# A four-layer attention kernel: queries of a quad projected in one piece, two norm statistics moved to another slot

## What is computed

```python
# block 0: self-attention with rotary q and k, a 128x128 mask; then cross-attention to 77 context tokens; then an MLP
x = x + g_msa * (attn(rope(q), rope(k), v, mask) @ attn_out_W)   # "l0", 128 keys, 16 heads of 8
x = x + g_x * (attn(qc, kc, vc, kv_mask) @ co_W)                 # "l0c", 77 keys
x = x + g_mlp * mlp(adaLN(x))
# block 1: routed experts over x and an attention to the context ("routed")
# block 2: cross-attention to 77 context tokens                    "l2"
# block 3: self-attention "l3s" (128 keys, no mask), cross-attention "l3c" (77 keys), MLP
```

## Time and profile before

| | |
|---|---|
| median of 3 runs | 1057.93 us (1056.93 to 1058.32) |
| the profiled execution | 1056.9 us |
| its span | 1055.1 us |
| mean granted TensorE clock | 0.985 of full |
| TensorE busy | 1011.1 us, 96% |
| VectorE, ScalarE, GpSimd busy | 773.0, 602.4, 677.2 us |

### The profile page before, as it was taken

One profiled execution on the slowest core, in us unless ns is written; L12 is line 12 of the kernel. 1 busy time (PEld: TensorE's weight loads), 2 busy tenths in 40 slices (PEclk: granted clock), 3 DMA queues, 4 the chain that ended last, 5 costly groups with the idle time before them and its releaser, 6 DMA issues.

```text
span 1055.1 us, 28781 instructions
## 1 busy us (share of the span) xinstructions
PE 1011.1 (96%) x11721; PEld 639.5 (61%) x11721; DVE 773.0 (73%) x1932; ACT 602.4 (57%) x858; POOL 677.2 (64%) x779
## 2 busy tenths in 40 slices
PE   7899999999999999999999799999999999999998
PEld 5345555656655776666776555655556666665576
DVE  7889988778885443777787779888998867777421
ACT  2144444566767455455554466666666677666762
POOL 6688888687985333111114689987889767688620
PEclk9699999999999999999999899999999999999999
DMA  6300000000000102000000000000000000000011
GB/s 218 119 2 2 21 14 13 12 22 22 12 22 22 40 31 99 13 7 8 7 7 19 7 14 2 2 2 2 1 2 2 1 3 2 2 2 2 2 40 40
DMA packets 9282, 22.76 MB, mean 22 GB/s; under 512 B 1392, under 2 KB 1648, under 8 KB 8768
## 3 DMA queue, kind: packets, MB, share of 16 engines
q1 hardware_dynamic: 9152, 20.94, 5.7%
HBM read 18.77 MB, written 2.15 MB: 20 GB/s over the span
## 4 chain that ended last, share of the span: by engine, by line
PE 81%; DVE 10%; issue 4%; ACT 2%; POOL 2%; DMA 0%; SPq 0%; DVEq 0%; POOLq 0%; ACTq 0%
PE weighed L707 13%; PE scores L679 11%; PE row_scores L642 8%; PE scores L903 6%; PE weighed L730 5%; DVE negmax L1221 5%; PE quads L578 4%; PE scores L597 4%; PE quads L589 3%; PE scores L692 3%; PE row_scores L903 3%; PE quads L604 3%; PE row_scores L720 2%; PE scores L720 2%; PE weighed L920 2%
## 5 line engine op out<-in xcount | busy, mean ns | idle before, releaser
L1221 DVE TENSOR_REDUCE negmax<-row_scores 128x8 f32<-128x616 f32 (+1 forms) x312 | 298.8, 958 | 80.2 <-PE row_scores L642 62.3
L1730 ACT ACTIVATE p<-scores 128x1024 f32<-128x1024 f32 (+1 forms) x253 | 249.1, 1019 | 159.4 <-PE scores L692 131.9
L679 PE MATMUL scores<-qblk,work 32*77 32x512 f32 (+1 forms) x1256 | 203.8, 612 | 5.0 <-ACT p L1730 3.3
L1912 POOL TENSOR_TENSOR kblk_r<-work,pack_const 128x308 fp32r<-128x308 f32 (+1 forms) x160 | 133.6, 836 | 64.5 <-PE row_scores L642 48.7
L707 PE MATMUL weighed<-p,v 77*32 77x128 f32 (+1 forms) x5120 | 172.9, 276 | 0.3
L1902 POOL TENSOR_TENSOR qblk<-work,pack_const 128x512 f32<-128x512 f32 x160 | 166.0, 1038 | 0.0
L642 PE MATMUL row_scores<-kblk_r,qr 32*128 32x308 f32 (+1 forms) x624 | 141.6, 445 | 20.1 <-DVE negmax L1221 16.9
L707 PEld LDWEIGHTS weighed<-p,v 77*32 77x32 f32 (+1 forms) x5120 | 130.1, 109 | 36.8 <-issue 29.0
L642 PEld LDWEIGHTS row_scores<-kblk_r,qr 32*128 32x128 f32 x624 | 62.0, 186 | 107.5 <-issue 69.6
L1949 POOL TENSOR_TENSOR attn<-nat,rden 128x128 f32<-128x128 f32 x160 | 65.6, 410 | 55.6 <-DVE rden L1251 54.5
L692 PE MATMUL scores<-nblk,select 32*77 32x512 bf16 (+1 forms) x628 | 95.4, 375 | 0.0
(11 more groups left out here) (327 smaller groups left out, 1868.6 us busy)
## 6 DMA issues: line engine op xcount, KB each, us to landing
shared<-gates_hbm SPq DMA_DIRECT2D x24, 256.0 KB, 3.1
shared<-in_ctx_tok SPq DMA_DIRECT2D x15, 154.0 KB
pack_w_l<-in_w_l SPq DMA_DIRECT2D x1, 2058.5 KB, 11.4
x<-in_x_tok SPq DMA_DIRECT2D x8, 256.0 KB, 6.0
out_x<-x SPq DMA_DIRECT2D x8, 256.0 KB, 2.0
layers_w<-in_w_l SPq DMA_DIRECT2D x1, 1289.0 KB, 9.4
ctxT<-in_ctxT SPq DMA_DIRECT2D x1, 1232.0 KB, 9.6
layers_w<-in_w_ada SPq DMA_DIRECT2D x1, 582.0 KB, 4.9
```

Of the source, the lines that this page charges most:

```text
L679: mm = e.matmul(score_banks(n, g // 2)[0:nk, g % 2, :], k_of[q % 3][at, s * nk:(s + 1) * nk], qblk[n % 2][at, :], start=layer.mask != "qk" ...
L1221: e.tensor_reduce(negmax[q % 2][:, 2 * h:2 * h + 2, s * NJ:(s + 1) * NJ], row_banks(n, h)[:, :, 0:NJ * nk].rearrange("p g (j k) -> p g j k ...
L1730: e.activation(p[n % 2][0:nk, 8 * h:8 * h + 8, :], score_banks(n, h)[0:nk].rearrange("p g (j q) -> p (g j) q", j=NJ), ACT.Exp, bias=hide, ...
L1912: e.tensor_tensor(kblk_r[n % 2][:, 0:NJ * nk].rearrange("p (j k) -> p j k", j=NJ), k_of[q % 3][:, s * nk:(s + 1) * nk].unsqueeze(1).to_bro ...
```

## The change

Two edits. First, at a wide place 3 the whole of quad qi+3's queries is projected in `quad_ahead`, in one piece of 512 columns, and nothing is left for `quad_work`. It touches 16 slots: the place 3 of quads 0 to 7 and of quads 24 to 31. Second, for norms whose `last` is from 3 to 31 and not of the other family, the slots of the four statistics go from `last-1, last-1, last, last` to `last-3, last-3, last-1, last-1`. These are the norms in front of quads 5 to 11: one pair of statistics stays at place 1 (the other pair now), and one pair goes from place 2 (t = 6, 10, ..., 30) to the place 3 before it (t = 3, 7, ..., 27). All these slots are in l0. Root and normalisation stay where they were.

```diff
@@ slots_of
     elif last < 4 * NB:
-        at = [last - 1, last - 1, last, last]
+        at = [last - 3, last - 3, last - 1, last - 1]
@@ quad_ahead
                     if cl == 3 and qi + 3 in quads:
-                        project_q(qi + 3, slice(0, 2))
+                        project_q(qi + 3)
@@ quad_work
-                    if cl == 3 and qi + 3 in quads:
-                        project_q(qi + 3, rest)
+                    if cl == 3 and qi + 3 in quads and not is_wide(t):
+                        project_q(qi + 3)
```

## The result

The changed kernel takes 1060.80 us (median of 9 runs, 1059.27 to 1062.14), the kernel before beside it 1057.66 us (9 runs, 1056.59 to 1058.86). The ratio is 1.0029 with a 95% interval of 1.002 to 1.0038: slower by 3.1 us, where 1060.6 was forecast.

A forecast was written before the change was run, and what follows sets the result against it. l0 was taken as set by VectorE and its round trip with TensorE. +0.66 (l0) + 2.04 (l3s) = +2.7 us on the profiled 1056.9 is 1059.6, plus 1.0 for the median: 1060.6 us, range 1058.9 to 1062.2.

The forecast's parts named there:

- Leg B of l0: l0, second row scores of place 3 to those of place 0: VectorE full, +0.68 us, quads 0 to 4.
- Leg A of l0: l0, up to the second row scores of place 3: TensorE sets it, 0.51 us shorter in quads 2 to 4.
- Quad 5 without `rotate`: In l0: -0.50 us up to place 3's second row scores, -0.18 after them, -0.68 together.
- quads 6 and 7: l0, TensorE busy without a gap: plain saving, -0.25 us each, statistics of t = 27 hidden.
- The split at place 2: l0, cast and subtraction (`split_max`) beside GpSimd: 1.29 us in place of 1.57, gaining nothing.
- the rival of the missed turn: Place 2 of l0, quads 2 to 5: subtraction ends 1.0 us later, +2.0 us, total 1062.6; chance 0.12.
- The price of the whole projection ahead: Place 3, ahead of the second row scores: whole projection 1.01 us of TensorE, half 0.63, so +0.38 us.
- l3s: Only the projection changes: 0 in quads 24 and 25, +0.38 each in 26 to 29, sum +2.04 us.
- The rival in which only l3s is hidden: Even stretches of quads 26 to 31 have 0.4 us of slack: 0 to -0.25 each, about 1057.6; chance 0.21.
- the one in which TensorE is the bound everywhere: Both layers: each of 16 slots gives 0.25 us, four gaps of 0.48 close, 1052.0; chance 0.17.
- Quads 30 and 31: l3s, shorter row scores of 77 keys behind them: between -0.25 and +0.38, taken as +0.26 each, 0.52 us.
- leg A of l3s: l3s, to place 3's second row scores: VectorE sets quads 24 and 25, TensorE 26 to 29, +0.38 us each.

The follow-up runs named there:

- e2: Kernel before, with the whole projection of queries ahead only in l3s; 1060.12 us, ratio 1.002.
- e5: Kernel before, with the whole projection behind the second row scores and `turn_max` in quads 26 to 31, nothing ahead of them; 1059.73 us, ratio 1.0014.
- e4: Kernel before, with the second half of the projection put ahead of `weigh` in l3s; 1062.56 us, ratio 1.004.
- e1: Kernel before, with only the statistics moved and projections left in two halves; 1057.98 us, ratio 0.9995.
- e8: Kernel before, with l0 statistics at places 3, 0 and twice 1, each slot's first in VectorE's wait, whole projection in quads 6 and 7; 1055.10 us.
- e7: Kernel before, with the edits of e6 and e5 together; 1057.86 us, ratio 1.0.
- e9: Kernel before, with the edit of `gap_stats` alone: only the first of two statistics at place 1 of l0 in VectorE's wait; ratio 1.0001.
- e3: Kernel before, with the whole projection of queries ahead only in l0, statistics left at place 2; 1056.62 us, ratio 0.9988.
- e6: Kernel before, with statistics moved only for quads 6 to 9 and the whole projection ahead only in quads 6 and 7; 1056.96 us, ratio 0.9985.

## Why the prediction came out

**The sum.** Forecast +2.7 in the changed slots, measured +3.14, and the same 3.14 between the medians. The table has each term, of both signs, within 0.17 us of its forecast, and most are above it. That the two 3.14 agree to the hundredth is luck: the interval of the medians reaches from 2.1 to 4.0, and had the kernel before started as e2 did, quad 0 would show about 0.26 more. That 1060.6 lies 0.2 from 1060.80 is in part luck too: the kernel before was 0.27 faster beside the changed one than the 1057.93 that the forecast set out from, which hides part of the 0.44 missing in the sum.

**Leg B of l0 is VectorE's.** Right. (In l0 the second half stood not behind `weigh`, as the order given ahead of the prediction has it, but in front: L578 at 153.91, L707 at 154.54, in quad 4. The sums don't use this order.) The leg grew by 0.66 us (5.63 against 4.97) for 0.68 forecast, in quads 0 to 4, and the time that TensorE no longer needs there turned into its waits of 0.32 and 0.76 us. This is where the gain of the larger matmul went.

**Leg A of l0 is TensorE's after the change.** Right: no gap in front of the second row scores. Quads 1 to 4 are 0.01 to 0.05 above the forecast, by the price below.

**Quad 5 without `rotate`, quads 6 and 7.** -0.69 for -0.68, by two errors that cancel: leg A gave 0.44 for 0.50 (the price below), leg B 4.71 - 4.47 = 0.24 for 0.18. In quads 6 and 7 it is -0.21 twice for -0.25, and the statistics at t = 27 cost nothing, as forecast.

**The split at place 2.** 1.28 us for 1.29. The cast and the subtraction took their turns in GpSimd's stretch at the two boundaries named, in quads 1 to 5 alike (0.95 to 0.98 us, then 0.36), so the rival of the missed turn (+2.0) is out. The Trainium skill (SBUF — State Buffer, Who interferes with whom) has the lock held for a whole instruction, and the trace agrees: the cast lasted 0.97 us here and 0.62 in the earlier trace rows, with the same operands. That a waiting VectorE instruction got the very next turn was seen in these rows; no run was made to test it.

**The price of the whole projection ahead.** This term was mis-sized. The forecast took 1.01 us from a place with 77 keys and so +0.38 us more than a half; at the places of the change it is 789.61 - 788.55 = 1.06 us, and so +0.43. It isn't the 128 keys: in e5 the same piece with 128 keys behind `weigh` cost 1.00 (788.64 to 789.64). Halves show the same: 0.63 between the `shift`s, but 789.24 - 788.66 = 0.58 behind `weigh` of l3s, where the forecast had 0.63. Ahead of the row scores the piece stands between the two `shift`s, behind `weigh` of l3s it doesn't; no run took these apart, and why it costs 0.05 us more there stays open. Four quads of l3s cost 0.42 to 0.44 each for 0.38, and it also took 0.04 of the 0.25 saved in quads 6 and 7.

**l3s.** The mechanism was right: nothing in quads 24 and 25, where the row scores start 1.07 us after the projection as before; the full delay in quads 26 to 29, for a chain behind the second row scores that is full. e2 has it alone, and e4 shows that the chain passes on any delay. The rival in which only l3s is hidden, and the one in which TensorE is the bound everywhere, ask for slack of 0.4 us in it; e2, e4 and the sum of the changed kernel exclude both.

**Quads 30 and 31.** +0.26 for each was a value between two bounds, and neither quad had it: +0.18 and +0.43. In quad 31 the row scores of place 0 followed those of place 3 after 3.50 us before and after the change. Timeline of TensorE after it:

```profile
873.19 1.12 PE L578 MATMUL quads<-work,layers_w 128*128 128x512 f32 x2
...
874.25 0.41 PE L642 MATMUL row_scores<-kblk_r,qr 32*128 32x308 f32 x2
...
877.75 0.40 PE L642 MATMUL row_scores<-kblk_r,qr 32*128 32x308 f32 x2 [0.51 <-DVE negmax L1221]
```

It waits 0.51 us for VectorE there, so the half saved behind `weigh` buys nothing and the 0.43 is paid in full. In quad 30 this leg was 3.75 us and is now 861.97 - 858.48 = 3.49, so TensorE had set it, and 0.26 comes back. I had treated the two as one.

**What I got wrong behind the prediction** is e5. "Second row scores with no gap" was read as "TensorE sets the leg". It was even: VectorE's maximum before it frees the banks at most 0.03 us before TensorE arrives. In the changed kernel this doesn't show, because TensorE comes later still; it decides as soon as TensorE gets faster. The forecast's leg B was weighed for both engines, its leg A of l3s for one.

## What to carry to other kernels

Where two engines pass one buffer back and forth, cut the loop at each hand-over and ask for both engines when they can be there. A merge of two matmuls that saves TensorE time lost here where the larger one stood ahead of the hand-over and nothing waited there (quads 26 to 29), and it was worth its plain saving where TensorE had no partner to wait for (quads 6 and 7). Before work is moved off a stretch, find a wait of the same engine that is long enough to take it: the same statistics, moved into a full stretch, gained nothing (e1), and spread so that the first of each slot falls into a wait, gained about 3.1 us (e8 by its slots, without the 0.4 of quads 6 and 7 and the 0.26 of the start; 2.7 us in all between the medians).

Two edits that use the same gap can't be priced one by one: -0.2 and -0.66 us made +0.81 together.

## What the runs showed of the hardware beside this

**The clock at the start differs from run to run.** Windows from 50 to 54 us of the kernel before and of the changed kernel: length, busy of PE, PEld, DVE, ACT, POOL, then the granted clock.

```profile
50.00:54.00 4.00, 4.00 (x51) 1.78 (x50) 3.04 (x5) 1.02 (x1) 2.43 (x2) 0.78 0.00 0
```

```profile
50.00:54.00 4.00, 4.00 (x31) 1.58 (x30) 3.04 (x5) 0.59 (x1) 2.17 (x2) 0.50 0.00 0
```

TensorE is busy all 4 us in both, at a mean granted 0.78 and 0.50 of full: the second is 1.2 GHz throughout, the first has some of 2.4 GHz, with 51 matmuls done against 31. In the next 4 us both have 0.99 or more. Over all the profiled executions here: the three with 0.50 (the changed kernel, e2, e8) reached place 3 of quad 0 1.0 to 1.3 us later than the kernel before; e7 and e9, with 0.51 and 0.63, 0.7 us later; the five with 0.71 to 0.83 (e1, e3, e4, e5, e6) between 0.15 earlier and 0.27 later. e2 changes nothing before l3s, and still is among the late ones, so this is no effect of an edit. What sets the moment at which the clock rises stays open.

There is a second such place, at the start of phase 1, which no edit here touches. Between two of its projections (L578 at 592.28 and 608.28 in the kernel before) lie 16.0 us in that kernel, the changed one, e3, e5, e6 and e9, but 16.7 in e1, 17.7 in e2 and e8, and 15.35 in e4 and e7. In the window from 590 to 596 us the mean granted clock is 0.72, 0.81 and 0.72 in e1, e2 and e8, and 1.00 in all others. A single pair of executions can thus differ by over 2 us for reasons that aren't the edit's, of 3.1 that were to be measured here. The sum over the changed slots leaves out all of this but what quad 0 takes over from the start (up to 0.26 us).

**The same cast takes 0.97, 0.78 or 0.62 us** (changed kernel, e8, before, quad 4), as GpSimd's instruction beside it ends, and 0.15 at 188.76 of the kernel before, where GpSimd runs no 1.04 us instruction beside it but a division that starts at 188.74. An average duration of such an operation says little; its end can be read off GpSimd's list.
